# An attention and experts kernel on one core: TensorE's loop over the batches written out, and the copies of o moved from VectorE to ScalarE

## The reference

```python
x = L0_attn_x                                   # (8, 512, 128)
xn = _layernorm(x, axis=-1)
# attention: q, k, v of 16 heads of 8; softmax(q k^T / sqrt(8) + causal) v, then w_out and b_out
# experts: sum over the two chosen e of combine[t, e] * (silu(xn wg_e) * (xn wu_e)) wd_e, plus the shared one
x = x + attention(xn) + experts(xn)
```

## Time and profile before

| | |
|---|---|
| time, median of 3 runs | 583.13 us (580.03 to 585.15) |
| the profiled execution: its time | 582.21 us |
| its span, from first to last instruction | 580.4 us |
| granted TensorE clock, mean | 0.983 |
| TensorE busy | 518.6 us (89%) |
| VectorE busy | 432.2 us (74%) |
| ScalarE busy | 327.9 us (56%) |
| instructions | 17,518 |
| GpSimd busy | 229.7 us (40%) |

### The profile page before, as it was taken

One profiled execution on the slowest core, in us unless ns is written; L12 is line 12 of the kernel. 1 busy time (PEld: TensorE's weight loads), 2 busy tenths in 40 slices (PEclk: granted clock), 3 DMA queues, 4 the chain that ended last, 5 costly groups with the idle time before them and its releaser, 6 DMA issues.

```text
span 580.4 us, 17518 instructions
## 1 busy us (share of the span) xinstructions
PE 518.6 (89%) x6840; PEld 327.7 (56%) x6840; DVE 432.2 (74%) x851; ACT 327.9 (56%) x447; POOL 229.7 (40%) x201
## 2 busy tenths in 40 slices
PE   2679999998999989899899998999989999999995
PEld 1345554666556754576446764566645665467643
DVE  4879977897858966697657967589656886579713
ACT  5422487354873468444793457734685347844593
POOL 2025700586006830369004770068402692047700
PEclk9979999998999999999999999999999999999997
DMA  9786035700366005640159003670046401690000
GB/s 265 214 232 147 3 105 148 215 2 9 113 187 179 2 11 175 192 111 1 67 165 254 5 10 112 168 199 1 11 147 208 123 1 64 160 259 4 11 20 20
DMA packets 46906, 62.71 MB, mean 108 GB/s; under 512 B 6672, under 2 KB 30448, under 8 KB 46832
## 3 DMA queue, kind: packets, MB, share of 16 engines
q1 hardware_dynamic: 44124, 58.34, 35.6%
q10 hardware_dynamic: 2708, 3.24, 1.8%
HBM read 45.18 MB, written 15.34 MB: 104 GB/s over the span
## 4 chain that ended last, share of the span: by engine, by line
PE 59%; DVE 15%; issue 10%; ACT 9%; DMA 3%; POOL 3%; SPq 1%; DVEq 0%; ACTq 0%
PE banks L712 7%; ACT probs L976 7%; PE banks L578 7%; DVE neg_max L1270 7%; PE banks L580 6%; PE banks L579 6%; PE banks L614 6%; PE banks L594 6%; PE banks L682 5%; PE banks L595 3%; PE banks L596 3%; DVE probs L1246 2%; PE banks L532 2%; POOL hid_lo L1065 2%; DMA wqk_sb<-in_wqkT 1%
## 5 line engine op out<-in xcount | busy, mean ns | idle before, releaser
L1270 DVE TENSOR_REDUCE neg_max<-banks 128x2 f32<-128x1024 f32 (+7 forms) x240 | 178.2, 792 | 33.6 <-PE banks L605 33.3
L1065 POOL TENSOR_TENSOR hid_lo<-probs,hid_hi 128x512 fp32r<-128x512 f32 x85 | 109.6, 1289 | 227.7 <-ACT hid_hi L920 227.3
L976 ACT ACTIVATE probs<-banks 128x1024 f32<-128x1024 f32 x144 | 138.6, 1027 | 25.1 <-PE banks L695 24.9
L913 ACT ACTIVATE probs<-banks 128x512 f32<-128x512 f32 (+1 forms) x112 | 66.9, 598 | 149.8 <-PE banks L580 149.4
L1057 POOL TENSOR_TENSOR probs<-probs,cb 128x512 f32<-128x512 f32 x88 | 113.0, 1284 | 89.8 <-ACT probs L913 89.2
L1246 DVE TENSOR_TENSOR probs<-probs,banks 128x512 f32<-128x512 f32 (+1 forms) x112 | 76.1, 681 | 36.7 <-POOL probs L1057 28.3
L578 PE MATMUL banks<-x_hi,w_hi 128*128 128x512 f32 (+1 forms) x224 | 96.3, 430 | 5.1 <-DVE probs L1246 4.4
L580 PE MATMUL banks<-x_hi,w_lo 128*128 128x512 f32 (+1 forms) x224 | 90.4, 404 | 0.0
L579 PE MATMUL banks<-x_lo,w_hi 128*128 128x512 f32 (+1 forms) x224 | 89.7, 400 | 0.0
L920 ACT ACTIVATE hid_hi<-probs 128x512 fp32r<-128x512 f32 (+1 forms) x96 | 60.3, 628 | 40.6 <-DVE probs L1246 40.5
L712 PE MATMUL banks<-probs,v_op 64*32 64x512 f32 (+7 forms) x2048 | 79.5, 409 | 2.2 <-issue 2.2
(11 more groups left out here) (137 smaller groups left out, 562.8 us busy)
## 6 DMA issues: line engine op xcount, KB each, us to landing
cb<-c_dram SPq DMA_DIRECT2D x31, 256.0 KB, 3.9
q_op<-q_dram SPq DMA_DIRECT2D x15, 512.0 KB, 6.6
k_op<-k_dram SPq DMA_DIRECT2D x15, 512.0 KB, 7.8
cb<-c_dram SPq DMA_DIRECT2D x16, 224.0 KB, 4.6
q_dram<-q_parts SPq DMA_DIRECT2D x8, 384.0 KB, 3.1
k_dram<-k_parts SPq DMA_DIRECT2D x8, 384.0 KB, 3.1
cb<-c_dram SPq DMA_DIRECT2D x16, 192.0 KB, 3.8
cb<-c_dram SPq DMA_DIRECT2D x15, 160.0 KB, 4.0
```

Source lines behind the costliest of these rows:

```text
L976: nc.scalar.activation(probs[:, 2 * home_of(n):2 * home_of(n) + 2, :], ring[:, at:at + 2, :], ACT.Exp).then_inc(exp_done, 1)
L1065: nc.gpsimd.tensor_tensor(hid_lo[0:n, k % 3, :], hid[k % 3][0:n, :], hid_hi[0:n, k % 3, :].bitcast(F32), ALU.subtract).then_inc(hid_lo_don ...
L1270: return nc.vector.tensor_reduce(out, in_, AX.X, ALU.max, negate=True)
```

## The change

TensorE's loop becomes a Python loop, so that its five passes stand in the queue one after the other and each wait has a constant. The 48 increments a batch of `apart` are gone from TensorE's queue, in the batches that were written out before too; SyncE and GpSimd keep theirs. The loops of the other four engines stay. `take_o` leaves VectorE's queue and stands in ScalarE's, between its SiLUs of k = 0 and k = 1, as two `ACT.Copy` activations. The last batch's `last_take_o` stays on VectorE.

```diff
@@ project_v_and_logits, scores, transpose_maxima, scores_t, weigh_v (TensorE)
-                apart(pe, pe_passed)
@@ TensorE, the order of the batches
-            with pe.Fori(1, NB - 2) as i:
+            for i in range(1, NB - 2):
                 attend(i, True)
                 experts_and_maxima(i + 1, i, True)
@@ ScalarE
+            def take_o(i, a):
+                act.wait_ge(pv_done, PV_ALL * i + PV_ALL)
+                nc.scalar.activation(o_sb[:, a, :], nat[:, a, :], ACT.Copy).then_inc(o_taken, 1)
+
             def experts(b, i, front):
                 for k in range(NT):
+                    if k == 1 and i is not None:
+                        take_o(i, 0)
+                        take_o(i, 1)
                     silu(b, k)
@@ VectorE
-            def take_o(i, a):
-                dve.wait_ge(pv_done, PV_ALL * i + PV_ALL)
-                nc.vector.tensor_copy(o_sb[:, a, :], nat[:, a, :]).then_inc(o_taken, 1)
@@ VectorE, experts_and_maxima
                     for m in range(PAIRS_AT[k]):
-                        if k == 1 and m == 1:
-                            take_o(i, 0)
-                            take_o(i, 1)
```

More of the change, by code:

```diff
@@ L331, in block_kernel @@
         last_summed = sem("last_summed")
-        pe_passed = sem("pe_passed")
         pool_passed = sem("pool_passed")
```

## The result

The changed kernel takes 567.1 us (median of 4 runs, 566.55 to 567.59), the kernel before 583.13, so 16.0 us less. The ratio is 0.973, with a 95% interval of 0.968 to 0.977: 2.7% less time. All medians here leave out runs that lasted over 1.5% more than the fastest run of the same kernel (one of the kernel before, 594.55 us). The profiled execution took 567.31 us with a span of 565.5, so against that of before (582.21) it is 14.9 us less. The forecast was 571.9, in a range of 565 to 576.

A forecast was written before the change was run, and what follows sets the result against it. TensorE was taken as the bound. From the profiled 582.2 us: less 10.2 for the loop and 1.3 for the copies, plus 0.3 for the operand load, gives 571.0; the median's 0.9 makes 571.9, range 565 to 576.

The forecast's parts named there:

- 2.2 us for the copies: Part of the range's lower end: extra gain allowed for moving the copies of o, from their upper bound of 3.5 us.
- 4.5 for late waits: Four TensorE waits a batch, product 0.14 us behind the releaser: at most 4.5 us from removing increments; sum took 0.
- What bounds the kernel: TensorE, busy 62.95 to 63.06 us a pass at full clock; only its standing still can be shortened.
- The loop, 10.2 us: TensorE's passes 2 to 5, written out, should last as long as pass 1, entered without a jump: 10.2 us less.
- The increments, 0 us: Taking the 48 increments a batch out of TensorE's queue was put at 0 us in the sum.
- the row nearest to the increment itself: TensorE between consecutive units of scores: eight products and four masks take 0.30 us, an increment between, no hole.
- rival (c): Straight TensorE code meets late instruction fetches, 5.1 us a pass, giving 597 us, slower by 2.6%; chance 0.05.
- The copies, 1.3 us: Copies of o moved to ScalarE: VectorE's maxima 0.18 us earlier in seven batches, TensorE's wait 1.38 becomes 1.20.
- Rival (a): SyncE's operand load replaces the stall in passes 2 to 5: 0.3 us likely, up to 4; full size 573 to 576, chance 0.12.
- Rival (b): Increments held back TensorE's weight loads at tile size changes: up to 15 us more gain, 557 to 566; chance 0.10.

The follow-up runs named there:

- the other pairing: The changed kernel with the 48 increments a batch put back, against the changed kernel: 576.65 us, 9.6 more.

## Why the prediction came out as it did

The direction was right, and so was the loop as a reason; the time is in the range, at its lower side: 16.0 us by the medians where 11.2 were forecast, 14.9 by the profiled executions. That it is in the range is in part luck. The lower end allowed 2.2 us for the copies and 4.5 for late waits; the copies brought nothing beyond their 1.3, the late waits some 0.3 us a pass, and what filled the gap was something that the prediction didn't have.

- **What bounds the kernel: right.** TensorE's 63.0 us of work a pass didn't change, and every gain in the passes was a piece of the time it stood still. Outside the passes the clock gave something back, which the sum had at nothing: TensorE's busy time fell from 518.6 to 516.4 us, at a mean clock of 0.990 in place of 0.983.
- **The loop, 10.2 us: the mechanism is shown in the passes, the size is open.** With the loop alone written out the passes gave 9.0, and one jump by itself 2.2. The kernel as a whole gained 6.5, with an interval of 1.6 to 10.4 that doesn't quite exclude 10.2. Pass 1 was a fair trial for the passes, but it had no hole by luck: with the same queue it took 67.04 us in another run, and straight code with increments has holes of 2 to 3 us at some places. The sum treated one profiled execution as if its straight part were always like that.
- **The increments, 0 us: this is the term that failed.** The prediction took 0, "the row nearest to the increment itself is the one without a hole". With the loop written out they cost 10.3 us (577.46 to 567.15) and 9.6 in the other pairing; what they cost in a kernel that keeps the loop was not measured, only that taking them out of its straight half brings 3.4. Where no wait is late the row was right: 0.33 us with one and with none. The bound for late waits was on the page, 0.14 against the 0.06 of after, or 0.08 * 4 = 0.3 a pass; the passes got 0.3 us shorter on average from that and from fewer holes (329.9 to 328.3). What no bound held is the rest: with increments behind the waits the queue has holes, in which nothing that the profile shows holds TensorE up, with the clock at 0.50 behind them. That was neither in the sum nor a rival; I had put late instruction fetches into rival (c), as a cost of the loop written out, without seeing that the other edit decides whether such holes appear.
- **The copies, 1.3 us: right in the trace, not measurable.** 0.19 a pass against 0.18, and a wait for the maxima of 1.2 in place of 1.4 with the copies alone. The medians with and without them are 567.1 and 567.15. Cost on ScalarE: none, with slack for as much again.
- **Rival (a), operand load: real and small.** 0.40 us in pass 2. Its cause was named wrongly: it stayed with SyncE's loop written out. What makes it come and go from run to run is open.
- **Rival (b), weight loads held back: refuted** by the 0.33 with and without an increment.
- **Rival (c), late fetches in straight code:** holes exist, but at a few places and not several in each pass, and in the kernels without increments behind waits none was over 0.9 us. That a hole is a late fetch is inferred: the trace has no row for a fetch.

By the experiments the sum reads: loop 6.5, increments 10.3, copies 0, together 16.8 against 16.0 measured; the first two are each uncertain by 3 us or more. Shown is that the place of the increment against its wait decides (11.1 us for moving it). That the front end stops at it is the explanation that fits all runs; the trace doesn't show the front end. Why a fetch would be late just there wasn't tried. The holes stand behind some 4 us of transfers, at 223 to 272 GB/s ahead of the one at 425 us and at 236 to 262 ahead of those in the last batches, so that transfers delay it is a rival to be tested; they alone don't make a hole, as the kernel after has them without one.

No version is better than the changed kernel by more than 0.3%; those between 565.55 and 566.7 differ from it mostly ahead of the first pass, whose start varies from 141.9 to 143.9 us.

## What to carry to other kernels

A loop's first pass, entered without a jump, gives an estimate of what writing the loop out will bring; subtract it from the others. Take more than one profile for it, and look whether the straight code has holes of its own. When an engine's instruction stands between a wait and the work that needs it, ask not only what it costs but what it keeps the engine from taking in meanwhile; put it ahead of the wait, or let the work carry the wait. A stall of TensorE can cost more than its length, because the clock behind it may be at the lower level: behind the holes of 2.38 and 3.33 us it was, behind the stalls of up to 2.0 at the jumps of the kernel before the passes kept 1.00.

## What was not expected of the hardware

One increment on TensorE's queue costs nothing where work is streaming (0.33 us from product to product with and without it); with four in a row the further ones cost 45 ns each on average, and 0.14 us each at one such place. 128 of them at the head of the program moved TensorE's first product from 11.15 to 20.50 us. In straight code a group of eight small products was cut by a hole of 2.38 us, another by 3.33, with the granted clock at 0.50 in the windows behind them. The Trainium skill ("Runtime: NRT & Kernel Launch", "Instruction fetch mechanics") has it that a block's boundary in straight code is mostly hidden. No trace here shows a boundary. If the holes are late fetches at such boundaries, the kernels without increments behind waits agree with it (no issue wait over 0.9 us behind the first product) and those with them don't (2.38 and 3.33).
